# The last stage of an attention and feed-forward kernel: where tiles are turned, when six of them are loaded, and the order of two operations of VectorE

## What is computed

```
x = x + xattn(layernorm(x), ctx_512, Wq, Wkv_expand, Wout)
x = x + ffn(layernorm(x), weight)

def ffn(x, weight):                      # x: 8192 rows of 1024
    w_fp8, w_scale = quant_e4m3(weight)  # scale from the largest magnitude, 448 at most
    x_fp8, x_scale = quant_e4m3(x)       # one scale for all rows
    return bfloat16((x_fp8 @ w_fp8.T) * x_scale * w_scale)
```

## Time and profile before

| | us |
|---|---|
| median of 3 runs (1724.70 to 1724.78) | 1724.76 |
| the profiled execution, its own time | 1724.69 |
| span of its profile | 1722.5 |
| TensorE busy (share of the span) | 1700.2 (99%) |
| VectorE busy | 1331.8 (77%) |
| ScalarE busy | 674.7 (39%) |
| GpSimd busy | 186.7 (11%) |
| feed-forward stage: first `linear` matmul to the end of the span | 1485.2 to 1722.5 |

### The profile page before, as it was taken

The page is one execution under the profiler, slowest core; times in us unless marked ns, Lnnn a source line. Parts: engine busy times, 40 slices in busy tenths (PEclk is TensorE's granted clock), DMA queues, the critical chain, the costliest instruction groups (busy, mean ns, idle before and its releaser), DMA issues.

```text
span 1722.5 us, 27606 instructions
## 1 busy us (share of the span) xinstructions
PE 1700.2 (99%) x11437; PEld 805.3 (47%) x11437; DVE 1331.8 (77%) x1908; ACT 674.7 (39%) x643; POOL 186.7 (11%) x151
## 2 busy tenths in 40 slices
PE   8899999999999999999999999999999999999998
PEld 4544444445444544454445444544454444544444
DVE  8886687788866887778777877787778775877786
ACT  7632232223322332233223322332234222799985
POOL 0000000000000000000000000000000002355565
PEclk9999999999999999999999999999999999999999
DMA  9346654553545544545454455544454553699997
GB/s 356 103 123 153 153 102 124 134 142 87 129 122 130 114 121 115 137 113 129 122 128 123 105 126 130 123 111 123 122 129 110 123 111 73 242 327 328 324 275 213
DMA packets 395370, 260.81 MB, mean 151 GB/s; under 512 B 349312, under 2 KB 351872, under 8 KB 395008
## 3 DMA queue, kind: packets, MB, share of 16 engines
q1 hardware_dynamic: 395264, 259.31, 57.0%
HBM read 113.25 MB, written 67.11 MB: 105 GB/s over the span
## 4 chain that ended last, share of the span: by engine, by line
PE 86%; DVE 9%; ACT 2%; issue 2%; DMA 1%; POOL 0%; SPq 0%; DVEq 0%; ACTq 0%; POOLq 0%
PE ps_all L783 36%; PE ps_all L799 33%; PE ps_all L958 12%; DVE m_buf L1397 3%; PE ps_all L766 3%; PE ps_all L736 1%; DVE tile_space L1466 1%; DVE hsum L1460 1%; DVE tile_space L1408 1%; DVE tile_space L1454 1%; PE ps_all L808 1%; PE ps_all L875 1%; DVE hmax L1449 1%; ACT tile_space L1071 1%; ACT tile_space L1075 1%
## 5 line engine op out<-in xcount | busy, mean ns | idle before, releaser
L783 PE MATMUL ps_all<-m_buf,tile_space 128*128 128x504 f16 x3072 | 667.6, 376 | 1.5 <-DVE tile_space L1454 1.5
L799 PE MATMUL ps_all<-n_buf,tile_space 128*128 128x512 f16 x3024 | 667.4, 379 | 0.3 <-DMA tile_space<-tile_space 0.3
L783 PEld LDWEIGHTS ps_all<-m_buf,tile_space 128*128 128x128 f16 x3072 | 297.7, 98 | 352.4 <-issue 7.9
L799 PEld LDWEIGHTS ps_all<-n_buf,tile_space 128*128 128x128 f16 x3024 | 293.1, 98 | 356.8 <-issue 7.0
L603 POOL TENSOR_TENSOR rstd_x<-veps_x,minus_half 128x1 f32<-128x1 f32 x64 | 35.2, 551 | 1386.9 <-DVE veps_x L1421 1386.9
L1079 ACT ACTIVATE tile_space<-tile_space,neg_mean 128x1024 f32<-128x1024 f32 x56 | 64.5, 1152 | 279.3 <-DVE neg_mean L1486 279.3
L1075 ACT ACTIVATE tile_space<-tile_space,score_scale 128x1024 f32<-128x1024 f32 x64 | 73.6, 1150 | 241.3 <-DVE tile_space L1454 241.3
L1071 ACT ACTIVATE tile_space<-tile_space 128x1024 f16<-128x1024 f32 x64 | 67.7, 1058 | 190.3 <-DVE tile_space L1466 190.3
L1408 DVE SCALAR_TENSOR_TENSOR tile_space<-tile_space 128x1024 f16<-128x1024 f32 x64 | 78.4, 1226 | 70.8 <-ACT tile_space L1071 70.8
L1460 DVE TENSOR_REDUCE hsum<-tile_space 128x16 f32<-128x1024 f32 x64 | 77.9, 1217 | 58.5 <-ACT tile_space L1075 58.5
L1403 DVE SCALAR_TENSOR_TENSOR tile_space<-tile_space 128x1024 f16<-128x1024 f32 x64 | 78.3, 1223 | 52.9 <-ACT tile_space L1065 52.9
(11 more groups left out here) (193 smaller groups left out, 1564.7 us busy)
## 6 DMA issues: line engine op xcount, KB each, us to landing
tile_space<-in_x_dram SPq DMA_DIRECT2D x128, 512.0 KB, 4.0
x_scratch<-tile_space SPq DMA_DIRECT2D x56, 512.0 KB, 3.1
m_buf<-x_scratch SPq DMA_DIRECT2D x32, 512.0 KB, 5.6
out_dram<-m_buf SPq DMA_DIRECT2D x32, 512.0 KB, 5.5
tile_space<-x_scratch SPq DMA_DIRECT2D x24, 512.0 KB, 5.8
out_dram<-tile_space SPq DMA_DIRECT2D x24, 512.0 KB, 5.5
m_buf<-in_L_xattn_Wq_dram SPq DMA_DIRECT2D x4, 1024.0 KB, 11.9
n_buf<-in_L_xattn_Wout_dram SPq DMA_DIRECT2D x4, 1024.0 KB, 13.1
```

Source lines behind the costliest of these rows:

```text
L783: mm = nc.tensor.matmul(ps_s[:, half * HALF:half * HALF + RH], left[:, ls, c * P:(c + 1) * P], m_buf[:, rs, c, half * RH:(half + 1) * RH], ...
L799: mm = nc.tensor.matmul(to[:, cols], left[:, ls, j * P:(j + 1) * P], right[:, rs, j, cols], start=(c == 0 and i == 0), stop=(c == CT - 1 a ...
```

## The change

Four things change.

1. Tiles 50 to 55 get places of their own, `late_x1`: four in `w8_raw` (free once the turned weights stand in `wo_t`), two in slots 8 and 9 of `tile_space`. SP loads them before step 0 of its loop, after waiting for `w8_turned` and `x_amax_turned`. `KEPT` is now 50, so the reloads end at step 34, and `HELD` is the old 56.
2. `BY_DMA` is 16: even tiles are turned by DMA from tile 32 on, and from there VectorE makes their scaled values.
3. In `quantise_pair` `copy_rt` stands behind the rounding of the odd tile, for all pairs from 8 to 15 (before, it stood ahead of it from pair 9 on).
4. Loops are written out where the pairs now differ, and the four filler matmuls ahead of the stage read a constant instead of `w8_raw`.

```diff
-        KEPT = T - TB
+        HELD = T - TB
+        KEPT = HELD - 6
+        late_x1 = [w8_raw[:].rearrange("p j c -> p (j c)")[:, i * 2 * H:(i + 1) * 2 * H].bitcast(F32) for i in range(4)] + [
+            tile_space[:, i, :] for i in (8, 9)]
-        BY_DMA = 24
+        BY_DMA = 16
...
         def x2_at(t, i):
-            return kept_x1[t - KEPT] if isinstance(t, int) and t >= KEPT else x2[i]
+            if isinstance(t, int) and t >= KEPT:
+                return kept_x1[t - HELD] if t >= HELD else late_x1[t - KEPT]
+            return x2[i]
...
+            sp.wait_ge(w8_turned, 16 * CT)
+            sp.wait_ge(x_amax_turned, 1)
+            for t in range(KEPT, HELD):
+                sp.dma_start(late_x1[t - KEPT], x1_dram[bass.ds(t * P, P), :]).then_inc(got_late, 16)
             for t in range(T - 1):
...
-                nc.tensor.matmul(ps_all[:, 3 * HALF:4 * HALF], ident_bf[:], w8_raw[:, k, 0:HALF], start=True, stop=True)
+                nc.tensor.matmul(ps_all[:, 3 * HALF:4 * HALF], ident_bf[:], ident_bf[:].unsqueeze(1).to_broadcast([P, HALF // P, P]), start=True, stop=True)
...
                 shifted(2 * k + 2, 0)
-                copy_first = not (known and (k >= BY_DMA or 2 * k < NATURAL + 2))
-                if copy_first:
-                    copy_rt(k, (i + 1) % 2)
...
                 rounded(2 * k + 2, 0, rows_buf[:, (i + 1) % 4])
-                if known and k == NATURAL // 2:
+                if not (known and (k >= BY_DMA or 2 * k < NATURAL)):
                     copy_rt(k, (i + 1) % 2)
                 if by_dma:
                     values(2 * k + 2, 1)
```

More of the change, by code:

```diff
@@ L275, in xattn_ffn_kernel @@
         y_half = sem("y_half")
+        got_late = sem("got_late")
         y_part = sem("y_part")
@@ L332, in x1_at @@
         def x1_at(t, e):
-            return kept_x1[t - KEPT] if isinstance(t, int) and t >= KEPT else x1[e]
+            return kept_x1[t - HELD] if isinstance(t, int) and t >= HELD else x1[e]
         def x2_at(t, i):
-            return kept_x1[t - KEPT] if isinstance(t, int) and t >= KEPT else x2[i]
+            if isinstance(t, int) and t >= KEPT:
+                return kept_x1[t - HELD] if t >= HELD else late_x1[t - KEPT]
+            return x2[i]
         def tile_of(n, parity):
@@ L496, in step @@
                 known = isinstance(t, int)
-                if not (known and (t == 0 or t > KEPT)):
+                if not (known and (t == 0 or t > HELD)):
                     sp.wait_ge(x1_ready, t + 1)
@@ L542, in _ @@
             for e in range(2):
-                sp.wait_ge(x1_stored[e], 16 * (KEPT // 2))
-            sp.wait_ge(x1_done, KEPT)
+                sp.wait_ge(x1_stored[e], 16 * (HELD // 2))
+            sp.wait_ge(x1_done, HELD)
             for t in (8, 9, 12, 13, 14, 15):
@@ L1247, in magnitudes @@
                     act.wait_ge(got_x1[i], (t - i) * (16 // X2) + 16)
+                elif t < HELD:
+                    act.wait_ge(got_late, 16 * (HELD - KEPT))
                 if isinstance(n, int) and n < ENTRY_TILES + 2:
@@ L1317, in _ @@
             step2(NATURAL - 5, NATURAL - 5)
-            with act.Fori(0, T // X2 - 2) as q:
+            with act.Fori(0, T // X2 - 3) as q:
                 for i in range(NATURAL - 4, NATURAL - 4 + X2):
                     step2(q * X2 + i, i % X2)
-            for t in range(T - 2 * X2 + NATURAL - 4, T):
+            for t in range(T - 3 * X2 + NATURAL - 4, T):
                 if t + AHEAD < T:
@@ L1521, in step @@
                 if not first:
-                    residual(t - 1, 1 - e, stored=not (known and (t < 3 or t > KEPT)))
+                    residual(t - 1, 1 - e, stored=not (known and (t < 3 or t > HELD)))
                 if here and not first:
@@ L1757, in values @@
                     dve.wait_ge(got_x1[t % X2], t // X2 * 16 + 16)
+                elif t < HELD:
+                    dve.wait_ge(got_late, 16 * (HELD - KEPT))
                 nc.vector.tensor_scalar(v_t[e], x2_at(t, t % X2), quant_a[:, t:t + 1], quant_b[:, t:t + 1], ALU.mult,
@@ L1826, in _ @@
                 first_pair(k)
[L1827 to L1832, removed]
+            for k in range(NATURAL // 2 - 1, T // 2 - 1):
                 quantise_pair(k // 4, k % 4)
```

## The result

| | before | changed |
|---|---|---|
| median of 20 runs each, same chip (us) | 1724.99 | 1728.48 |
| lowest to highest (us) | 1724.58 to 1726.78 | 1725.81 to 1730.42 |
| profiled execution, its own time / span (us) | 1724.69 / 1722.5 | 1727.40 / 1725.6 |

The ratio is 1.0018 with an interval of 1.0012 to 1.0024: 3.5 us slower by the medians, 2.7 us in the profiled pair, against a forecast of 1730.2 (+5.5). The sign holds and the range holds it. What follows asks whether the steps do. Seven single executions of the whole record (two of the kernel before, five in experiments 1, 9 and 11) took 1785 us or more and are left out of every ratio.

A forecast was written before the change was run, and what follows sets the result against it. TensorE, busy 99% of the span, was taken as the bound. The terms -3.5 - 0.3 + 4.5 + 4.8 = +5.5 us on the profiled 1724.69 gave 1730.2 us, slower; range 1722.5 to 1733.8 us.

The forecast's parts named there:

- Transposes, -3.5: TensorE, last stage: eight fewer groups of eight transposes at 0.44 us each, all on the path, save 3.5 us.
- The old waits, -0.3: TensorE's existing waits for its first even turns, 0.3 us in all, are replaced by the new stalls: -0.3 us.
- Six loads at nothing: Stage entry: six early loads, 7.8 us of DMA engines, are hidden in the DMA-idle stretch before 1500 us: 0.
- The first even turn, +4.5: Tile 32: SP issues the turn behind step 28's reload, at 1602.41; it lands at 1608.0, 4.5 us late (bounds 2.0 to 6.0).
- The next three turns, +4.8: Tiles 34, 36, 38: SP's loop takes 8.5 us per pair against TensorE's 6.91; three stalls of 1.6, 4.8 us (2.9 to 6.9).
- The copy at nothing: VectorE, pairs 8 to 15: the copy behind the rounding still ends before TensorE loads its weights: 0, 2 us at most.
- Scaled values on VectorE at nothing: Eight more pairs: VectorE makes scaled values, 1.38 us each in place of a 0.69 copy, hidden behind TensorE: 0.
- Rival B: One stall of 4.5 us, during which the queue drains; later turns land in time: +0.7 us, 1725.4; chance 0.14.
- Rival A: SP's queue is level with VectorE at step 29, so no first stall: 1720.9 to 1723.8 us; chance 0.20.

The follow-up runs named there:

- experiment 1: Changed kernel with even tiles turned by DMA only from tile 48 (BY_DMA back at 24), early loads and copy order kept: 1724.38 us.
- experiment 9: Changed kernel with even turns by DMA from tile 40 (BY_DMA at 20) and every reload one step later: 1722.91 us.
- experiment 11: Changed kernel with even turns by DMA from tile 36, reloads up to step 28 one step later, then one reload per pair of steps: 1723.44 us.
- experiment 2: Changed kernel with even turns by DMA from tile 40 (BY_DMA at 20): 1723.27 us.
- experiment 5: Changed kernel without the six early loads, these tiles being reloaded at steps 35 to 40 as before: 1732.65 us.
- experiment 3: Changed kernel with every reload one step later, into the slot whose store was issued two steps earlier: 1723.80 us.
- experiment 8: Changed kernel with reloads up to step 28 one step later and the last seven spread over steps 29, 31, 33, 35, 37, 39 and 40: 1724.12 us.
- experiment 7: Changed kernel with no reload at step 28 and the last seven reloads spread over steps 29, 31, 33, 35, 37, 39 and 40: 1729.40 us.
- experiment 12: Kernel before, with one edit: every reload one step later, into the slot of tile t - 2 instead of t - 1: 1724.81 us.
- experiment 4: Changed kernel with 16 filler matmuls on constants on TensorE ahead of its wait for the first even turn: 1726.44 us.
- experiment 6: Changed kernel with the copy of the turned tile ahead of the rounding again, as before: 1729.56 us.

## Why the prediction was right, and where it wasn't

The sum against the profiled pair: -3.5 for the transposes, +4.5 for the first stall, +1.9 for the slow pair behind it, +0.3 for tile 38: +3.2 us, where the spans differ by 3.1 and the executions' own times by 2.7.

- **Transposes, -3.5: right.** 64 instructions fewer; experiments 2 and 9 give 1.7 and 2.0 us for four groups worth 1.8 (with a wait of 0.7 in the first).
- **The old waits, -0.3: not there to be saved.** The earlier trace rows is a row of weight loads (PEld), which overlap the matmuls; the matmuls lose nothing, since the 296 of the earlier trace rows run through these tiles at 0.216 us each.
- **Six loads at nothing: right**, for the reason given. What they take away turned out worth 4.2 us by the medians (experiment 5), of which 2.8 can be placed; the prediction used it but didn't price it.
- **The first even turn, +4.5: right in mechanism and in size.** Issued at 1602.19 (1602.41 forecast), landed 6.0 us later (5.6), stall 4.51. Experiments 3 and 8 take SP's waits away and the stall falls to 0.66 and 0.49. One reading was off: the prediction has the reload of step 28 wait for a landing until 1601.93. In the trace before it follows the issue of its step's store (1600.68 + 1.20) by 0.05 us; the long wait, 2.9 us, is the one ahead of the reload of step 27, issued at 1598.75 behind a store whose issue ended at 1595.86. It changes nothing in the sum, but experiment 7, which takes out the reload of step 28 alone, rested on it and missed. SP's queue before:

```profile
1595.19 0.67 SPq L532 DMA_DIRECT2D out_dram<-tile_space  x1
1598.75 0.34 SPq L528 DMA_DIRECT2D tile_space<-x_scratch  x1
...
1600.68 1.20 SPq L532 DMA_DIRECT2D out_dram<-tile_space  x1
```

- **The next three turns, +4.8: the step that failed.** They cost 0.28 us, and the size of a term was wrong twice. First, the pair of steps was put at 7.20 + 1.33 = 8.5 us, with 7.9 as the lower bound; the landings came every 7.64. The 7.20 was read as SP's own pace with 0.15 us to spare. Experiment 12 shows that it held waiting which a turn can fill: SP's waits for landings shrink from 57.3 to 42.8 us (24.5 + 18.3) with the change, and nearly go with a one-line edit. The lower bound was none either: from tile 32 to tile 34 the queue is never empty, and its four transfers and two turns land in 6.81 us (1608.19 to 1615.00) where the busy shares had given 7.9. A store or reload lands 1.2 us behind the transfer before it there and a turn 0.9 to 1.0, so it was most of all the turn that was priced too high, at 1.33. That a share of busy time counts packets that lie on top of each other, as the prediction itself warned, would explain it; that isn't shown. Second, TensorE's need was taken as 6.91 us for each pair, though the first of them takes 8.78. With both: 3 x (7.64 - 6.91) - 1.87 = 0.3 us, the wait at tile 38.
- **Missing: the clock, +1.9.** The prediction priced the stall at its length alone. Experiment 4 keeps the clock up and gets 2.0 us back.
- **The copy at nothing: right** (a weight load waits 0.4 us once, no matmul does). The new order seems to help the first turn, by 0.7 us at its issue and 1.1 us in the medians, with overlapping intervals: experiment 6.
- **Scaled values on VectorE at nothing: right.** From 1632 us on TensorE has no wait for VectorE or DMA.

So the failed terms, 4.5 too much, 1.9 and 0.3 too little, explain the 2.3 us between forecast and sum (5.5 and 3.2). They pull opposite ways: that the forecast came as near as it did is in part luck. Rival B, one stall and then recovery, had the course of events right, though it gave the later turns' good timing to a drained queue, and with the clock beside it the size: 0.7 + 1.9 + 0.3. Rival A's deciding point was an issue 3.1 us before the weights of tile 32 are wanted. In the changed kernel these are wanted at 1603.26, and the issue at 1602.19 misses the point by 2.0 us. In experiment 3 they are wanted at 1604.36, and the issue at 1600.60 makes it by 0.7 us; the time is indeed no longer than before, but 3.1 us to land was too little (4.9), and 0.66 us of stall is left.

Settled in part only: why the later pairs of steps take longer than that 6.81 us. In the changed kernel the landings of even turns are 6.81, 7.77 and 8.34 us apart; in experiment 3, 7.03, 7.73 and 8.08. In the changed kernel SP waits there for sums that the stall has made late (the store at 1616.97 is issued 3.7 us behind the turn ahead of it), but experiment 4 has 2.9 us between two landings at 1616.25 and 1619.11 with the second issued at 1612.91, so that isn't all of it. One of the pauses shown further up lies between these two (1617.5 to 1618.7), and one in the longest of the changed kernel's intervals (1625.2 to 1626.5); 6.81 us and such a pause make up most of the 8.34. What makes the pauses stays open. Between 1606 and 1618.5 us the changed kernel's transfers land in the order of their issue, 0.9 to 1.3 us apart. The Trainium skill ("DMA: Bandwidth & Descriptors", "Queues, rings and completion order") has each DMA engine take its descriptors in ring order, but warrants no order of completion; the trace shows landings alone, and they agree with such an order in this stretch, with no exception. What a turn takes to land is then mostly the queue ahead of it; the gaps in that queue weren't tried by themselves.

## What to carry to other kernels

When one queue serves both bulk transfers and a transfer that the bounding engine waits for, look at what the queue waits for just ahead of the latter: a wait for a landing that was only just issued costs nothing while there is slack, and all of it once something urgent stands behind. Moving that wait one step away cost nothing where it wasn't needed (experiment 12) and gave 4.7 us where it was (experiment 3). And price a stall with what follows it, both ways: the idle time may bring the clock down, and the time lost gives later transfers room.

## What the runs showed that was not expected

- TensorE's granted clock was 0.50 behind idle times of 3.03 us (experiment 8), 4.51 (the changed kernel), 4.62, 5.42 and 5.86 us (experiments 7, 5 and 6), and stayed at 1.00 behind 1.70 and 1.13 us (experiment 5), 1.69 (experiment 7), 0.97 and 0.96 (experiment 4) and 0.66 (experiment 3). The 16 matmuls behind the idle time then took 4.92 to 5.96 us instead of 3.62.
- A turn of 256 KB lands in 3.0 us with nothing ahead of it, in up to 7.1 behind reloads, and in 6.7 behind two adjacent reloads and a pause. The latency of a transfer said more of the queue than of the transfer.
- A shorter landing alone bought nothing: the odd turns' median is 1.5 us less in experiment 12, and the time the same.
- With transfers in flight the DMA engines all but stop now and then, for 1.2 to 1.5 us at 7 to 60 GB/s, in the kernel before as in the changed one. One such pause ahead of a turn is as long as several of the waits that were argued about.
